# Transposes of silu times up ahead of the gathered rows, in a kernel of decayed linear attention and a mixture of 64 experts

## The reference

```python
scores = softmax(xf @ gate_w.T); topk_w, topk_idx = top_k(scores, 6)
# each of the 64 experts has up to 128 slots (CAP), filled with its tokens
gx = xp[buf_tok]                                      # (64, 128, 512)
gu = einsum('ech,ehi->eci', gx, gate_up_proj)         # 2 x 192 columns
g, u = split(gu, 2); hid = silu(g) * u
eo = einsum('eci,eih->ech', hid, down_proj) * buf_w[..., None]
routed = zeros.at[buf_tok].add(eo)
shared = silu(xf @ shared_gate_w.T) * (xf @ shared_up_w.T) @ shared_down_w.T
```

## Time and profile before

| | |
|---|---|
| median of 3 runs | 917.66 us (916.98 to 918.23) |
| the profiled execution, its own time | 912.01 us |
| span of its trace, first to last instruction | 910.3 us |
| mean granted clock of TensorE | 0.998 |
| busy over the span: PE, PEld | 886.9 us (97%), 733.4 us (81%) |
| busy over the span: DVE, ACT, POOL | 746.7 us (82%), 568.6 us (62%), 513.0 us (56%) |
| moved by DMA | 203.96 MB |

### The profile page before, as it was taken

One profiled execution on the slowest core, in us unless ns is written; L12 is line 12 of the kernel. 1 busy time (PEld: TensorE's weight loads), 2 busy tenths in 40 slices (PEclk: granted clock), 3 DMA queues, 4 the chain that ended last, 5 costly groups with the idle time before them and its releaser, 6 DMA issues. The chain is left out here.

```text
span 910.3 us, 15717 instructions
## 1 busy us (share of the span) xinstructions
PE 886.9 (97%) x4675; PEld 733.4 (81%) x4675; DVE 746.7 (82%) x1462; ACT 568.6 (62%) x1208; POOL 513.0 (56%) x540
## 2 busy tenths in 40 slices
PE   8999999999999999999999999999999999999997
PEld 7788887878888788777888888888888888877875
DVE  6997887979788897898858898898889898836776
ACT  5532535434353443535558888988988988836785
POOL 2002365566566656677434676776777767533665
PEclk9999999999999999999999999999999999999999
DMA  6343553436263333439567999999999999969963
GB/s 213 96 162 116 158 127 107 127 90 175 73 189 96 121 105 110 150 91 346 181 225 235 331 360 348 359 342 307 351 358 362 352 332 327 280 112 390 384 245 129
DMA packets 111635, 203.96 MB, mean 224 GB/s; under 512 B 18496, under 2 KB 50240, under 8 KB 110528
## 3 DMA queue, kind: packets, MB, share of 16 engines
q1 hardware_dynamic: 91024, 159.87, 50.6%
q0 software_dynamic: 19520, 35.75, 16.5%
q10 hardware_dynamic: 1008, 7.34, 2.1%
HBM read 143.03 MB, written 59.88 MB: 223 GB/s over the span
## 5 line engine op out<-in xcount | busy, mean ns | idle before, releaser
L1628 POOL DMA_INDIRECT slot_table<-tokens,slot_of x162 | 180.3, 1113 | 86.8 <-issue 50.4
L1662 POOL DMA_INDIRECT xg<-x_rows,table_sb x64 | 121.5, 1898 | 78.1 <-ACT eo L928 42.5
L1733 PE MATMUL bank<-x_hi,wqkv_hi 128*128 128x512 f32 x384 | 152.1, 396 | 0.8 <-DVE wqkv_lo L1035 0.8
L1733 PE MATMUL bank<-x_lo,wqkv_hi 128*128 128x512 f32 x384 | 150.2, 391 | 0.0
L1733 PE MATMUL bank<-x_hi,wqkv_lo 128*128 128x512 f32 x384 | 150.1, 391 | 0.0
L1673 POOL DMA_INDIRECT acc_rows<-eo,table_sb x64 | 113.8, 1778 | 52.1 <-DMA acc_rows<-eo,table_sb 21.8
L1467 DVE TENSOR_TENSOR wgu_lo<-wgu,wgu_hi 128x1536 fp32r<-128x1536 f32 x64 | 112.0, 1752 | 2.5 <-ACT wgu_hi L912 1.9
L912 ACT CAST wgu_hi<-wgu 128x1536 fp32r<-128x1536 f32 x64 | 94.5, 1478 | 1.6 <-issue 0.4
L1733 PE MATMUL bank<-wgu_hi,xgt_hi 128*128 128x384 f32 x256 | 91.4, 357 | 0.0
L682 ACT ACTIVATE e<-bank 128x512 f32<-128x512 f32 x64 | 38.0, 594 | 80.1 <-PE bank L1733 80.1
L1733 PE MATMUL bank<-wgu_lo,xgt_hi 128*128 128x384 f32 x256 | 85.8, 335 | 0.0
(11 more groups left out here) (207 smaller groups left out, 2333.2 us busy)
## 6 DMA issues: line engine op xcount, KB each, us to landing
wgu<-w_gu SPq DMA_DIRECT2D x64, 768.0 KB, 8.4
wdn<-w_down SPq DMA_DIRECT2D x64, 384.0 KB, 8.9
xres<-x SPq DMA_DIRECT2D x32, 256.0 KB, 3.4
x_turned<-x1t SPq DMA_DIRECT2D x32, 256.0 KB, 2.8
x_rows<-x SPq DMA_DIRECT2D x32, 256.0 KB, 3.0
acc_rows<-x SPq DMA_DIRECT2D x32, 256.0 KB, 3.2
fin<-acc_rows SPq DMA_DIRECT2D x8, 1024.0 KB, 11.8
odd<-acc_rows SPq DMA_DIRECT2D x8, 1024.0 KB, 13.5
```

Source lines behind the costliest of these rows:

```text
L1628: pool.indirect_dma_start(table_dram, bass.IndirectOffsetOnAxis(slot_of[:, i, k:k + 1], 0), tokens[:, i:i + 1], None, bounds_check=SLOTS - ...
L1662: pool.indirect_dma_start(xg[e % NXG][:, :], None, x1_dram, bass.IndirectOffsetOnAxis(table_sb[:, e:e + 1], 0), bounds_check=T - 1, oob_is ...
L1733: mm = pe.matmul(out_ap, a, b, start=first and i == 0, stop=final and i == len(products) - 1)
```

## The change

In PE's loop over the experts, `turn_rows(e + 2)` goes from ahead of the two transposes of `hid_e` to behind them. Its waits (for the gathered rows and for `xgt_lo_done`) move with it. Nothing else is changed.

```diff
                 for _ in range(fills_of[e]):
                     unit()
-                if e + 2 < NE:
-                    turn_rows(e + 2)
                 pe.wait_ge(hid_e_done, e + 1)
                 if e:
                     pe.wait_ge(het_lo_done, e)
                 for h in range(2):
                     mm = pe.transpose(ht_ps[:, h * P:(h + 1) * P], hid_e[e % 2][:, h * P:(h + 1) * P], ident[:, :])
                 mm.then_inc(ht_mm, 1)
+                if e + 2 < NE:
+                    turn_rows(e + 2)
             down(NE - 1)
```

## The result

The changed kernel takes 924.63 us in the median of 7 runs (923.44 to 926.34), the kernel before, run beside it, 918.53 us (916.98 to 921.96). The ratio is 1.0064, with a 95% interval of 1.0048 to 1.0080: slower by about 5.9 us. Forecast was 923.5 from 917.66, 5.8 us more.

The account below looks back on a forecast made before the run. The prediction took PE's matmuls in the expert loop to set the kernel's end, with DVE and ACT close to full. 19 x 0.33 = 6.3 us, less 0.5, on 917.66 gave 923.5 us, range 919.0 to 925.8.

Parts of the forecast that it names:

- What bounds the kernel: Expert loop, 475 to 805 us: PE, DVE and ACT nearly full; PE leaving the loop later delays the kernel's end equally.
- Cost at a second follower: Second expert behind one with a shared-part unit: row transposes wait behind `hid_e`, next gate-up 0.33 us later; 19 places, 6.3 us.
- X+1.08: Start of the gate-up behind a second follower, 1.08 us after `xgt_lo` ends (X); before the change X+0.75.
- One sign: Expected in the profile after: PE's pauses in second followers put down to `hid_e`, about 0.4 us longer each, some 19 times.
- Other places: Experts with a shared-part unit behind them, first and third followers: `hid_e` is ready when PE comes, so 0 cost.
- Gains: Seven first followers behind an up unit: product turned sooner, ACT's copy gains 0.07 us each, 0.5 us back; elsewhere 0.
- What could swallow the delay: PE's pauses for `het_lo` before down products in seven first followers might absorb delay; silu passes it on, so nothing counted.
- the low end: Five `het_lo` pauses swallow 1.7 us and each second follower costs 0.27: 2.9 us more in all, 920.6 us.
- The sum: Whole kernel: 6.3 us cost less 0.5 us gain, 5.8 us on 917.66, giving 923.5 us.
- No change: Rival: DVE or ACT sets the loop's pace, PE's delay is slack, only 0.5 us come back: 917.2 us; chance 0.11.
- Faster: Rival: sooner turned products speed ACT's copy and DVE's `het_lo`, 6.1 us gained, 911.6 us without the cost; chance 0.06.
- Lower clock: Rival: six transposes behind a longer pause lower PE's clock, 3.2 us per hundredth over the loop, 926.7; chance 0.02.

Follow-up runs that it names:

- run 1: Changed kernel, but second and third followers (second, third expert behind one followed by a shared-part unit) keep the old order: 911.84 us, ratio 0.9993 to the kernel before.
- run 2: Kernel before, with the new transpose order only in the 19 second followers (second expert behind one followed by a shared-part unit): 917.91 us, ratio 1.0058.
- run 6: Kernel before with the mixed order and, on ACT in first followers, the copy of the turned product ahead of scaling the last result (`eo`): 908.70 us, ratio 0.9959.
- run 5: Kernel before, with the row transposes' two waits swapped, split rows awaited before gathered rows: 910.76 us, ratio 0.9983.
- run 7: ACT's copy ahead of `eo` in first followers, with the kernel before's PE order (909.87 us, ratio 0.9971) and with the changed order everywhere (913.20 us, 1.0007).
- run 8: Kernel before with the mixed order, ACT's copy ahead of `eo` in first followers, and the row transposes' waits swapped: 907.25 us, ratio 0.9946.
- the mixed order: Product transposes first in fillers (experts with a shared-part unit behind them) and first followers, rows first in second and third followers; alone 911.84 us, ratio 0.9993.
- the last run: Changed kernel with the two waits before the product's transposes swapped, `het_lo` first and `hid_e` last: 918.94 us, ratio 1.0075 to the kernel before.

## Why the prediction was right

**What bounds the kernel.** Right. The loop's 5.55 us more are 5.9 in the time by the ratio (4.4 to 7.4 by its interval), with the stretch behind it unchanged, as the chain had it.

**Cost at a second follower.** X+1.08 was forecast and is measured in all 19; the sum behind it held in after: 0.40 to the end of `hid_e`, release 0.05 (595.47 to 595.52) and 0.63 from there to the gate-up (596.15) for the six transposes. The split of the 0.63 did not: the pair takes 0.28 and the four 0.35 (595.80), where 0.20 and 0.43 were forecast, each too far by 0.08 the other way. That these cancel was luck. The single row of expert 62, the only place where PE waited for `hid_e` right away, carried this. Before, `xgt_lo` ended the same 0.40 ahead of `hid_e`. So 0.33 was the right price, and 0.34 is the mean growth of the 13 outside the pairs behind up units. One sign was off: PE's pause ends 0.45 behind `xgt_lo` for 0.15, so it grew by 0.30, not by 0.4.

**Other places.** Fillers, first followers and third followers cost nothing, as said; run 1 shows it for the first two, and the profile of after for the third followers (0.00). There PE did wait for nothing: it came to the transposes 0.23 us or more behind the end of `hid_e`.

**Gains.** 0.07 in each of the seven first followers behind up units: run 1 has exactly this, 7 x 0.07, in the next expert. In the changed kernel the reason holds for 17 and 49 alone. In the other five run 2 has the same gain without the new order in first followers, by PE's lateness. The size of 0.5 was right, but for five of seven the reason is shown only where the second followers keep their order; that it came out the same was luck.

**What could swallow the delay.** The point with most doubt, and right. In after five of the seven pauses at `het_lo` are gone, and PE's list of waits alone would speak for the low end. But the second followers behind them grew by 0.66 to 0.69 (0.35 at expert 62), since silu starts with PE's gate-up and all of the chain on ACT and DVE behind it. In all 20 first followers silu starts 2.37 to 2.39 us behind the gate-up, before and after, and from there to the end of the next `xgt_lo` no place changed by more than 0.10. Run 2 shows the same shift of the pauses.

**The sum.** 5.8 forecast, 5.55 in the loop, 5.9 by the ratio. What is missing in the loop: the pair 61 and 62, which has no second follower with rows to turn, came out 0.09 shorter where 0.07 was counted, and the first followers are 0.01 shorter each (0.2 together).

**The rivals.** No change: DVE and ACT have as much work as before, and the delay went through, as their chain starts anew at each first follower with silu, at a fixed distance behind PE's gate-up. By the rule of the Trainium skill (Perfetto Trace Analysis, Identifying the Most-Contended Engine) DVE would be the engine to optimize first. Here the loop passes through all three engines: an earlier copy on ACT (run 6) and a quicker release on PE (run 5) both shortened it while DVE's busy time stayed at 286.6; no run took work off DVE, so what that is worth is not shown. Faster: the sooner product exists, but is worth 0.6 us by itself (run 1), and about 1.0 where the copy can start sooner (run 7). Lower clock: 1.00 in every stretch of the loop. DMA, which no rival named, has a share of 0.99 in the loop and still was no limit: the version of run 8 moves the same bytes in a loop 4.6 us shorter, at 330 GB/s for 325.

## What to carry to other kernels

When a listed wait is to be removed by doing something else first, ask whether the something else is ready sooner: here DVE makes it directly behind what was awaited, and the work put last, the four row transposes, no longer ran under the making of `hid_e`. A pause that shrinks in the list of waits is no gain until the next event that starts from this engine's own output comes sooner too; follow the distance from one round's first instruction to the next. And reorder by place: the same swap cost 0.33 us in second followers, nothing in fillers and most first followers, and gained 0.07 in seven of these, so the mixed order was the better one. Two gains that were each measured alone need not add up: runs 1 and 2 share one.

## What was not expected of the hardware

Of two waits ahead of PE's transposes in this kernel, the one that is satisfied last is better written first. With the awaited semaphore in the second place the transposes start 0.15 us behind the end of its releaser (the rows before, the product in the last run), in the first place 0.05 to 0.06 (the rows in run 5, the product in after). Of this, 0.06 is left at the start of the next gate-up, and 1.3 us over the loop. In the traces the wait written second is the separate instruction of 51 ns, and the one written first is carried by the weight load. That this instruction is the whole of the 0.10 is not shown; other counts of waits were not run.
